# A mixture-of-experts loop with its down product three steps behind the load in place of four, and the shared pieces spread from step 9 on

## The reference

```python
logits = jnp.einsum('btc,ec->bte', x, router_w)
top_vals, top_idx = jax.lax.top_k(logits, TOP_K)
gates = jax.nn.sigmoid(top_vals)
...
gu = jnp.einsum('nc,ech->neh', xf, gate_up_w)
gate, up = jnp.split(gu, 2, axis=-1)
h = jax.nn.silu(gate) * up
out_all = jnp.einsum('neh,ehc->nec', h, down_w)
moe = jnp.einsum('ne,nec->nc', w_full, out_all).reshape(Bb, Tt, C)
sg = jnp.einsum('btc,sc->bts', x, shared_gate_w)
su = jnp.einsum('btc,sc->bts', x, shared_up_w)
shared = jnp.einsum('bts,cs->btc', jax.nn.silu(sg) * su, shared_down_w)
return moe + shared
```

## Time and profile before

| what | us |
|---|---|
| median of 3 runs (563.98 to 569.35) | 568.07 |
| the profiled execution, whole | 568.54 |
| its span, first to last instruction | 566.7 |

### The profile page before, as it was taken

How to read it: one execution, slowest core, us unless ns; L and a number is a source line. 1 busy time by engine, 2 the same in 40 slices (tenths; PEclk the granted TensorE clock), 3 DMA queues, 4 the chain that set the end, 5 groups by cost and what they waited for, 6 DMA issues and landing times. The chain is left out here.

```text
span 566.7 us, 17496 instructions
## 1 busy us (share of the span) xinstructions
PE 469.9 (83%) x6139; PEld 348.1 (61%) x6139; DVE 409.6 (72%) x1247; ACT 296.8 (52%) x757; POOL 298.4 (53%) x588
## 2 busy tenths in 40 slices
PE   1977888888888888888999999999767999999810
PEld 1755666666666666545676676666544888888610
DVE  7566999999888888876889898987572434434337
ACT  2573665555556656524656656564424444444237
POOL 5543454444444334201358888777771577777720
PEclk9997999999999999969999999999989999999975
DMA  6626343455655655326233333332124334333158
GB/s 189 112 51 139 55 71 63 67 132 111 110 108 110 108 107 114 81 52 150 54 83 90 95 87 97 96 85 67 34 97 132 106 110 116 110 109 98 53 178 286
DMA packets 96006, 58.30 MB, mean 103 GB/s; under 512 B 24560, under 2 KB 92224, under 8 KB 95920
## 3 DMA queue, kind: packets, MB, share of 16 engines
q1 hardware_dynamic: 74448, 39.93, 30.2%
q10 hardware_dynamic: 16896, 7.34, 6.7%
q0 software_dynamic: 4576, 9.91, 5.1%
HBM read 20.76 MB, written 17.50 MB: 68 GB/s over the span
## 5 line engine op out<-in xcount | busy, mean ns | idle before, releaser
L507 POOL TENSOR_SCALAR veps<-mv 128x2 f32<-128x2 f32 x48 | 11.2, 232 | 144.9 <-issue 101.2
L1292 ACT ACTIVATE probs<-ps 128x512 f32<-128x512 f32 x128 | 73.3, 603 | 12.1 <-PE ps L1672 9.8
L613 POOL DMA_INDIRECT expert_in<-xn,sloti x64 | 65.5, 1023 | 17.6 <-issue 17.6
L1147 DVE TENSOR_TENSOR eh<-ps,sg 128x256 f32<-128x256 f32 x40 | 17.0, 425 | 59.8 <-ACT sg L1496 58.9
L772 DVE TENSOR_REDUCE nmax<-ps 128x8 f32<-128x512 f32 x64 | 42.5, 686 | 18.9 <-PE ps L1607 18.8
L666 POOL DMA_INDIRECT expert_out<-ey,xt x40 | 38.3, 957 | 27.0 <-DVE ey L1154 16.7
L772 DVE TENSOR_REDUCE mparts<-ps 128x8 bf16<-128x512 f32 x64 | 43.3, 687 | 6.7 <-PE ps L1662 6.3
L1607 PE MATMUL ps<-kbd,qs 96*64 96x128 bf16 x512 | 38.0, 293 | 4.5 <-DMA qs<-part 3.6
L2026 PE MATMUL ps<-wgu,turned 128*128 x160 | 41.3, 380 | 0.0
L1490 ACT COPY turned<-ps 128x512 f32<-128x512 f32 (+1 forms) x43 | 23.8, 554 | 28.5 <-PE ps L2019 23.2
L509 POOL TENSOR_TENSOR rstd<-veps,minus_half 128x2 f32<-128x2 f32 x48 | 35.8, 745 | 4.0
(11 more groups left out here) (248 smaller groups left out, 1360.2 us busy)
## 6 DMA issues: line engine op xcount, KB each, us to landing
kbd<-part SPq DMA_DIRECT2D x192, 32.0 KB
qs<-part ACTq DMA_DIRECT2D x93, 64.0 KB
xt<-expert_in SPq DMA_DIRECT2D x64, 72.0 KB
qs<-part SPq DMA_DIRECT2D x51, 64.0 KB
ck_scr<-wgu SPq DMA_DIRECT2D x6, 512.0 KB
ckbd<-ck_scr SPq DMA_DIRECT2D x16, 192.0 KB
kbd<-part SPq DMA_DIRECT2D x48, 64.0 KB
wgu<-in_L_ffn_gate_up_w SPq DMA_DIRECT2D x4, 512.0 KB, 4.0
```

What stands on the lines that cost most here:

```text
L613: pool.indirect_dma_start(xs, bass.IndirectOffsetOnAxis(sloti[b % 3][:, n:n + 1], 0), xn3[b % 3][:, n // TOPK, n % TOPK, :], None).then_in ...
L1292: a_.activation(probs[:, 2 * i:2 * i + 2, :], P2[i % 2][:, :].rearrange("p (j q) -> p j q", j=2), ACT.Exp, scale=SCALE).then_inc(s("probs" ...
```

## The change

The down product and its eviction move up one step: in step s they now treat step s-3. PE, DVE and the register load follow (the list of expert numbers that PE loads for a turn begins six tiles back in place of eight, so 20 numbers for a turn in place of 22, and the half of `turned` that the product reads is that of the step itself). The loop has three steps behind its last load, not four. And the pieces of the shared expert now come after the steps 9, 11, 13, 15, 17, 19, 21, 24, 26, 28, 30, 32, 34, 36 and 39.

```diff
-        FIRST_PIECE = 4
+        FIRST_PIECE = 9
...
-        PIECE_STEPS = [FIRST_PIECE + 5 * k // 2 for k in range(3 * (LATE - EARLY))]
+        PIECE_STEPS = [FIRST_PIECE + 15 * k // 7 for k in range(3 * (LATE - EARLY))]
...
                 def step(s, i, q):
                     if due(s - 1):
                         gated(s - 1, (q + 1) % 2)
-                    if due(s - 4):
-                        evict(s - 4)
-
-                step_loop(dve, step, 4, None, mixed)
+                    if due(s - 3):
+                        evict(s - 3)
+
+                step_loop(dve, step, 3, None, mixed)
...
-                    tiles = range(-8 if where else 0, RING - 2 if where < STEPS // TURNS else 0)
+                    tiles = range(-6 if where else 0, RING - 2 if where < STEPS // TURNS else 0)
...
                         gate_up(s - 1, (q + 1) % 2, 2 * q - 2)
-                    if due(s - 4):
-                        down(s - 4, (q + 1) % 2, 2 * q - 8)
-
-                step_loop(pe, step, 4, load_experts, mixed)
+                    if due(s - 3):
+                        down(s - 3, q % 2, 2 * q - 6)
+
+                step_loop(pe, step, 3, load_experts, mixed)
```

## The result

The kernel after takes 596.59 us (median of 6 runs, 593.31 to 600.0), the kernel before beside it 567.98 (6 runs). The ratio is 1.0519, with a 95% interval of 1.0486 to 1.0552: slower by 5.2%, and far above the range of the prediction. The span went from 566.7 to 594.7 us, the mean granted clock of TensorE from 0.961 to 0.949.

What follows compares the result with a forecast made beforehand. GpSimd's scatters bound it by a hair over TensorE; 5.8 + 0.5 + 3.8 + 0.4 put step 40 at 538.9 and the last scatter at 547.2 against 541.50. So 568.07 + 5.7 = 573.8 us, range 567.0 to 578.5.

Steps and rivals of the forecast that it cites:

- The bound: In the expert loop: GpSimd's scatters bound the kernel by a hair, 2.53 us a step against TensorE's 2.45.
- part 1: Start of the scatters: the first comes a step sooner, at 440.63; a gain of 2.4 us if POOL never waited again.
- Rival A: Whole kernel: POOL stays the bound and gets faster, with waits and register loads costing nothing; 565.7 us, chance 0.10.
- the moved product: Ahead of step 40: one extra down product is moved up from the tail, costing PE 0.44 us.
- Part 2: Steps 3 to 39: the down product waits for its own step's copy, 0.157 us a step, 5.8 us in all.
- the copy's wait: Steps 3 to 39: the down product's weight load waits for ScalarE's copy of that step's transposes, 5.8 us in all.
- the silu: In steps after a gate or up piece, ScalarE's silu delays the copy by 0.05, ten times: 0.5 us.
- rival C: Each loop step: the whole 0.265 us of the wait is lost, 4.0 us more, 577.8 us; chance 0.12.
- Part 3: Each eighth step: register loads show as 1.5 us of idle PE ahead of steps 8, 24 and 32; 3.8 us net.
- Rival B: Expert loop: the copy's wait counts but the register loads stay hidden; 570.0 us, chance 0.20.
- all shifts alike: Behind the last scatter: everything moves by the same 5.7 us as that scatter.

Runs made afterwards that it cites:

- experiment 5: Kernel after with the list begun eight tiles back and a shared-expert piece just ahead of each register load: 570.5 us, ratio 1.0032.
- experiment 1: Kernel after with PE's list of expert numbers begun eight tiles back instead of six (22 numbers, two unused): 575.64 us, ratio 1.0158.
- experiment 2: Kernel before with PE's list begun ten tiles back instead of eight (24 numbers, two unused): 589.71 us, ratio 1.0398.
- experiment 3: Two kernels: the kernel after with the list begun twelve or seven tiles back instead of six: 578.79 and 593.69 us, one run each.
- experiment 4: Two kernels: the kernel before with the new pieces alone, 565.72 us (566.21 timed again); the kernel after with the old pieces, 592.68 us.
- experiment 6: Kernel before with the new pieces and only the first three down products and evictions one step sooner: 568.05 us, ratio 1.0009.

## Why the prediction was wrong, point by point

**The bound and part 1 held.** The first scatter comes 3.47 after the transposes of step 3 (437.84 to 441.31), 3.45 was forecast. POOL ceased to be the bound. Rival A (565.7) fell: POOL waits for evictions, and experiment 5's 6.42 us less the 0.44 of the moved product are 0.16 a step over 37 steps, against the 0.08 from which A decides.

**Part 2 held.** The weight load of the down product starts 0.13 after the copy's end; steps without a piece take 1.90 (443.98 to 445.88 in the trace after). Forecast for the copy's wait, the silu and the moved product together: 5.8 + 0.5 + 0.4 = 6.7. Experiment 5 measures 6.42, or 7.1 with the idle 0.67 ahead of step 24 that its cover takes away. That speaks against rival C, which wanted 4.0 more.

**Part 3 is the step that failed: the price of the register load.** The prediction put it at 1.70 us, between loads of 8 and of 22 numbers in the earlier trace rows. It measured 4.97. A piece of 1.72, which was to cover such a load, left 3.14 idle ahead of step 16. The form of the step was right: from the copy's end to the next transposes 5.43 pass, 4.98 of them the load, so 0.45 around it where 0.29 + 0.19 = 0.48 were put. But the duration came from rows that all had lists beginning at a multiple of four, and the list of the kernel after begins six back. I took the price as set by the number of numbers, and 0 to 1.86 as bounds. Lists from 8 and 12 back against 6, 7 and 10 back (experiments 1 to 3) show that the place sets it: 0.08 to 0.09 us a number in the former (1.88/22, 2.15/26, 0.99/12; the first list, 14 from place 0, has 0.11, 1.53/14), 0.25 in the latter (4.97/20, 5.21/21, 5.98/24). No row of the trace before holds a load from such a place, so no row could have given its price. The fault was to treat it as one that the trace shows, with two ends close together, instead of as an unknown whose upper end stays open.

**A second term was missing: the clock.** The prediction named a clock under 1.00 in the loop as a sign of error, and it came. Against experiment 1, which differs in nothing but the list, the loop is 19.44 longer (121.88 against 102.44). The four steps behind which a load stands (7, 15, 23 and 31), from their transposes to those of the next step, take 6.66, 6.93, 6.64 and 6.95 in the kernel after and 3.73, 3.71, 3.53 and 3.64 in experiment 1: 12.6 us of longer loads. The gaps shown above say the same: four of 17.13 in all, against three of 4.65. The steps behind three of these gaps are longer too (from step 8 to 10 8.09 against 5.56, 24 to 25 5.15 against 3.65, 32 to 33 6.17 against 3.72): 6.5 us at half clock. Together 19.1 of 19.44.

**With the price of the earlier trace rows the sum holds.** Experiment 1 is the change with such loads: step 40 at 538.90 (forecast 538.9), last scatter 547.40 (547.2), 575.64 us (573.8). That the places agree so closely is in part luck: in that execution step 3 began at 436.46, 0.72 ahead of the 437.18 from which the forecast counts, and the loop took 102.44 where the sum makes 101.7. The gaps cost 4.80 (102.44 less 97.64), three of 1.5 were forecast: the loads are of 22 numbers and 1.88, not 1.70. **Rival B** (570.0) fell by the same run, in which three gaps of 1.46 to 1.67 stand. The rule of the Trainium skill that was weighed for it ("TensorE: Matmul & The Clock Gate", "Engine queue depths") doesn't cover a register load in this stream. The 570.0 come about only where a piece is put ahead of each turn: experiment 5, 570.5.

**The end.** From step 40 to the last scatter 8.51, forecast 3.2 + 5.05 = 8.25. Behind the last scatter "all shifts alike" was not quite right: 1.27 us more. Before, SyncE's read back began 2.34 after the last scatter's issue (541.50 to 543.84), after 3.93 (568.23 to 572.16).

The error of 22.8 us (596.59 less 573.8) is thus 12.6 for the loads, 6.5 for the clock and 1.3 at the end; 2.4 is left in small terms, 0.7 of it the later start of step 3.

No version is measurably faster than the kernel before. The new pieces alone have the lowest medians, and both their intervals hold 1.

## What to carry to other kernels

When a change moves the start of something that is read in bulk, price it as a new operation: compare the place it begins at with the place of every row that you take a duration from, and if they differ, hold its price for unknown. Here two numbers that nobody needs, ahead of the list, are worth 21 us. And a gap of a few us on TensorE may cost more than its length: look at the granted clock behind it.

## What the runs showed of the hardware

**A register load depends on where its list begins.** From a multiple of four numbers 22 took 1.88 us; from other places 20 took 4.97. Four more numbers cost 0.27 (26 against 22), about as much as a single one from another place (0.25), as if four were taken at a time in the one case and one in the other. That reading was not tried further. The Trainium skill, "Runtime: NRT & Kernel Launch", section "Instruction fetch mechanics", puts a register load at about 200 ns a register even in bulk; that page of the skill has such loads come from HBM, while the list here lies in SBUF (`tile_row`). The 0.25 of the lists from 6, 7 and 10 is of that size; those from 8 and 12 are at less than half. By the page's figure the list of 20 would take 4.0 us, an estimate nearer to the measured 4.97 than the forecast's 1.70; but the 22 numbers of the earlier trace rows would take 4.4 by it, an estimate too, and took 1.86.

**Half the clock behind a gap.** After idle gaps of 4.59, 4.57 and 4.83 us the kernel after ran PE at a granted clock of 0.50 to 0.52 for 5.86, 3.55 and 5.41 us, its lower level of 1.2 GHz. After the gap of 3.14 us it stayed at 1.00, 2.4 GHz, and experiment 1 with gaps up to 1.7 had 1.00 through the loop. The length of the gap alone doesn't tell: in experiment 2, behind one of 2.80 that ended at 478.54, the clock was 0.50 from 479.80 on. What else decides was not tried.

**The last scatter's landing.** From the issue of the last scatter to the read back it took 2.34 us before and 2.34 to 2.80 in the traces of experiments 2 to 6, but 3.93 after and 4.5 in experiment 1. The two kernels of experiment 3 and the second of experiment 4, which differ from the kernel after only in the list or in the pieces, have 2.35 to 2.80, so the longer time need not belong to the change. What makes the difference was not tried.
